# Eight relations around one x in a row of the projection table, read back five vectors at a time

## The reference

```
h_proj = einsum('nd,rde->rne', x, relation_weight)
att    = sum(h_proj[etype, src] * tanh(h_proj[etype, dst] + edge_attr), -1)
a      = softmax of att over the edges of one dst
h_nb   = segment_sum(x[src] * a, dst)
x1     = layernorm(x + leaky((x + h_nb) @ res_w1.T) + leaky((x * h_nb) @ res_w2.T))
feat   = x1 / out_degree
out    = layernorm(x1 + segment_sum(feat[src], dst) / in_degree)
```

## Time and profile before

| | us |
|---|---|
| median of 3 runs | 12504.19 (12502.96 to 12504.48) |
| profiled execution | 12504.09 |
| its span | 12502.3 |
| table stage ends (first load of the next) | 406.11 |
| first gather of the attention stage | 410.66 |
| first instruction of the node stage on VectorE | 8249.73 |
| first gather of the mean stage | 8446.5 |
| POOL / DVE / ACT / PE busy | 9106.9 / 4974.7 / 2167.4 / 1355.6 |

### The profile page before, as it was taken

How to read it: one execution, slowest core, us unless ns; L and a number is a source line. 1 busy time by engine, 2 the same in 40 slices (tenths; PEclk the granted TensorE clock), 3 DMA queues, 4 the chain that set the end, 5 groups by cost and what they waited for, 6 DMA issues and landing times. The chain is left out here.

```text
span 12502.3 us, 36138 instructions
## 1 busy us (share of the span) xinstructions
PE 1355.6 (11%) x4902; PEld 711.9 (6%) x4902; DVE 4974.7 (40%) x4627; ACT 2167.4 (17%) x1796; POOL 9106.9 (73%) x9773
## 2 busy tenths in 40 slices
PE   9311111110101111111111111140000000000001
PEld 3100000000000000000000000040000000000001
DVE  4455555555555555555555555561111111111113
ACT  4111111111111111111111111122222222222221
POOL 1577777777777777777777777757777777777776
PEclk9655555555555555555555555555555555555555
DMA  9422222222222222222222222211222222222222
GB/s 403 174 80 79 79 79 79 80 79 80 79 80 79 80 79 79 79 79 79 79 79 79 79 79 79 77 41 51 53 52 53 52 53 53 52 53 52 53 52 50
DMA packets 456359, 998.94 MB, mean 80 GB/s; under 512 B 189300, under 2 KB 242276, under 8 KB 443412
## 3 DMA queue, kind: packets, MB, share of 16 engines
q0 software_dynamic: 356272, 519.14, 18.2%
q1 hardware_dynamic: 62004, 271.05, 5.6%
q10 hardware_dynamic: 38064, 208.54, 4.2%
HBM read 629.48 MB, written 368.55 MB: 80 GB/s over the span
## 5 line engine op out<-in xcount | busy, mean ns | idle before, releaser
L1044 POOL DMA_INDIRECT gy<-ytab,idx x3125 | 2948.3, 943 | 999.6 <-issue 952.1
L817 POOL DMA_INDIRECT gs<-table,idx_s x3125 | 2953.3, 945 | 971.3 <-issue 971.3
L820 POOL DMA_INDIRECT gd<-table,idx_d x3125 | 2948.0, 943 | 951.3 <-issue 951.3
L1077 DVE TENSOR_TENSOR_SCAN run<-keep,add 128x1664 f32<-128x1664 f32 x125 | 452.9, 3623 | 3015.1 <-ACT keep L1101 3015.1
L868 DVE TENSOR_TENSOR banks<-banks,gd 128x1600 f32<-128x1600 f32 x125 | 229.0, 1832 | 3430.4 <-DMA gd<-table,idx_d 3430.4
L1006 PE MATMUL banks<-hi,lo 128*128 128x392 bf16 x3125 | 803.4, 436 | 6984.7 <-DVE hi L855 6984.7
L855 DVE TENSOR_TENSOR hi<-banks,digit 128x9800 bf16<-128x9800 f32 x125 | 1294.3, 10354 | 0.0
L972 ACT ACTIVATE banks<-banks 128x1600 f32<-128x1600 f32 x125 | 186.0, 1488 | 4912.5 <-DVE banks L868 4912.5
L1099 ACT COPY add<-gy 128x1600 f32<-128x1600 f32 x125 | 400.4, 3203 | 2474.2 <-DMA gy<-ytab,idx 2474.2
L1006 PEld LDWEIGHTS banks<-hi,lo 128*128 128x128 bf16 x3125 | 381.4, 126 | 7406.7 <-DVE hi L855 7033.6
L982 ACT COPY rowbuf<-run 128x1625 f32<-128x1625 f32 x125 | 410.2, 3282 | 776.4 <-DVE run L895 776.4
(11 more groups left out here) (184 smaller groups left out, 2402.7 us busy)
## 6 DMA issues: line engine op xcount, KB each, us to landing
table<-rows SPq DMA_DIRECT2D x98, 1536.0 KB, 9.4
sums<-rowbuf ACTq DMA_DIRECT2D x125, 825.0 KB, 3.7
ef<-in_edge_attr_dram SPq DMA_DIRECT2D x125, 800.0 KB, 4.9
sums<-rowbuf ACTq DMA_DIRECT2D x125, 800.0 KB, 3.5
gs<-table,idx_s POOLq DMA_INDIRECT x3125, 2.6
gd<-table,idx_d POOLq DMA_INDIRECT x3125, 2.4
gy<-ytab,idx POOLq DMA_INDIRECT x3125, 2.4
ytab<-y SPq DMA_DIRECT2D x7, 448.0 KB, 3.5
```

What stands on the lines that cost most here:

```text
L817: pool.indirect_dma_start(out=gs[:, s, g, :], out_offset=None, in_=table, in_offset=bass.IndirectOffsetOnAxis(ap=idx_s[:, s, g:g + 1], axi ...
L820: pool.indirect_dma_start(out=gd[:, s, g, :], out_offset=None, in_=table_third, in_offset=bass.IndirectOffsetOnAxis(ap=idx_d[:, s, g:g + 1 ...
L1044: pool.indirect_dma_start(out=gy[:, s, g, :], out_offset=None, in_=ytab, in_offset=bass.IndirectOffsetOnAxis(ap=idx[:, s, g:g + 1], axis=0 ...
L1077: nc.vector.tensor_tensor_scan(run[:, :, :].rearrange("p w t -> p (w t)"), keep[:, :, :].rearrange("p w t -> p (w t)"), add[:, :, :].rearr ...
```

## The change

- The table row is now eight relations around one x: [r0 r1 r2 r3 x r4 r5 r6 r7], 576 floats, four rows a node. Storage shrinks from 48 to 36 vectors a node. The copies of x shrink from 16 to 4 a block: VectorE two, ScalarE one, GpSimd one.
- A gather for the source takes five vectors: either [r0..r3, x] or [x, r4..r7]. VectorE multiplies and sums all five (x too) and picks the right one by three bits of the relation, in three predicated copies; a fourth, over 25 x 64 elements, brings x to one place. `edge_rows` has 11 short operations instead of five, and the three bits are kept until `back`.
- The node of block b in partition j is now j*98 + b, so x is loaded with one long piece per partition; the store of a block goes to 128 places that lie 98 blocks apart. For the node stages x is read again in the old order (node b*128 + j), by SyncE at the head of the attention node stage.
- Weights: even quarters of a row on partitions 0 to 63, odd ones on 64 to 127, loaded by eight DMAs; the matmuls of a block alternate between the halves, each with a contraction of 64 rows. The clearing of the lower half is gone.
- In the table stage only the first 50 columns of src, dst and type are loaded; the rest comes at the head of the attention stage. The rest of x is held until the weights are in.
- Clears at the head of both edge stages shrink to the columns that are read, and ScalarE no longer waits for them. The last chunk makes no indices.

```diff
-        table = nc.dram_tensor("table", (NPAD * R // 2, 3 * D), F32).ap()
+        table = nc.dram_tensor("table", (NPAD * R // 8, 9 * D), F32).ap()
+        table_vec = table.rearrange("a (b d) -> (a b) d", b=9)
...
-            nc.vector.scalar_tensor_tensor(out=idx_s[:, s, :], in0=src_sb[:, at], scalar=float(R // 2),
-                                           in1=half[:, :], op0=ALU.mult, op1=ALU.add)
+            nc.vector.scalar_tensor_tensor(out=idx_s[:, s, :], in0=src_sb[:, at], scalar=float(9 * R // 8),
+                                           in1=near[:, :], op0=ALU.mult, op1=ALU.add)
...
+                    sp.dma_start(xs[0:P - 1, 0:FIRST, :], x_rows[:, 0:FIRST, :]).then_inc(x_first, 16)
...
+                    sp.wait_ge(w_in, 128)
+                    sp.dma_start(xs[0:P - 1, FIRST:, :], x_rows[:, FIRST:, :]).then_inc(x_in, 16)
...
-                    sp.dma_start(src_sb[:, 0:T], src.rearrange("(p t) -> p t", p=P)).then_inc(idx_in, 16)
+                    sp.dma_start(src_sb[:, 0:SOON], src_v[:, 0:SOON]).then_inc(idx_in, 16)
...
+                        sp.dma_start(table_by_part[:, bass.ds(b, 1), :],
+                                     rows[:, s:s + 1, :, :].rearrange("p o r c -> p o (r c)")).then_inc(stored[s], 16)
...
+                            u, h = k // 2, k % 2
+                            nc.tensor.matmul(ps_p[k][:, :], xbT[64 * h:64 * h + D, s, :],
+                                             w_all[64 * h:64 * h + D, 2 * u:2 * u + 2, :, :].rearrange("d q c e -> d (q c e)"),
...
+                        vec = gs[:, s, :, :].rearrange("p g (c d) -> p g c d", c=5)
                         nc.vector.tensor_tensor(prod[:, :, :, :], arg.unsqueeze(2).to_broadcast([P, G, 2, D]),
-                                                gs[:, s, :, :].rearrange("p g (c d) -> p g c d", c=3)[:, :, 0:3:2, :],
-                                                ALU.mult).then_inc(ef_free, 1)
+                                                vec[:, :, 0:5:4, :], ALU.mult)
+                        nc.vector.tensor_tensor(vec[:, :, 1:4, :], arg.unsqueeze(2).to_broadcast([P, G, 3, D]),
+                                                vec[:, :, 1:4, :], ALU.mult).then_inc(ef_free, 1)
...
+                        nc.vector.tensor_reduce(att_of[:, 0:5:4, :].rearrange("p c g -> p g c"), prod[:, :, :, :], AX.X, ALU.add)
+                        link.then(nc.vector.tensor_reduce(att_of[:, 1:4, :].rearrange("p c g -> p g c"), vec[:, :, 1:4, :], AX.X, ALU.add))
+                        link.then(nc.vector.copy_predicated(att_of[:, 0:4, :], right[:, s, :].unsqueeze(1).to_broadcast([P, 4, G]),
+                                                            att_of[:, 1:5, :]))
+                        nc.vector.tensor_copy(side, right[:, s, :])
+                        link.then(nc.vector.copy_predicated(att_of[:, 0:2, :], high[:, s, :].unsqueeze(1).to_broadcast([P, 2, G]),
+                                                            att_of[:, 2:4, :]))
...
+                        link.then(nc.vector.copy_predicated(gs[:, s, :, 4 * D:5 * D],
+                                                            side.unsqueeze(2).to_broadcast([P, G, D]), gs[:, s, :, 0:D]))
...
+        xs = sb(ctx, "xs", [P, NB, D])
+                sp.wait_ge(x_pad, 1)
+                sp.dma_start(xs[:, 0:NB - 1, :], x[0:(NB - 1) * P, :].rearrange("(b j) d -> j b d", j=P)).then_inc(x_in, 16)
...
+                    if not later(i):
+                        dve.wait_ge(x_in, 32)
```

More of the change, by code:

```diff
@@ L539, in gnn_program @@
         half = sb(ctx, "half", [P, G], I32)
+        quad = sb(ctx, "quad", [P, G], I32)
+        near = sb(ctx, "near", [P, G], I32)
+        right = sb(ctx, "right", [P, 2, G], I32)
+        low = sb(ctx, "low", [P, G], I32)
+        high = sb(ctx, "high", [P, 2, G], I32)
         odd = sb(ctx, "odd", [P, 2, G], I32)
@@ L552, in gnn_program @@
         tail = sb(ctx, "tail", [P, RW])
+        SOON = 2 * G
+        src_v, dst_v, type_v = (v.rearrange("(p t) -> p t", p=P) for v in (src, dst, etype))
         def edge_rows(link, c, s):
@@ L711, in _ @@
                 def _(act):
-                    act.dma_start(w_all[0:D, :, :], rel_w.rearrange("r d e -> d r e")).then_inc(w_in, 16)
+                    w_v = rel_w.rearrange("(q h c) d e -> h q d c e", h=2, c=4)
+                    for h in range(2):
+                        for q in range(RQ):
+                            act.dma_start(w_all[64 * h:64 * h + D, q, :, :], w_v[h, q]).then_inc(w_in, 16)
                     def take_x(b, k, s):
@@ L721, in quarters @@
                         take_out(act, nc.scalar.copy, 1, b, s, i)
-                        nc.scalar.copy(rows[:, s, RP - POOL_DUP - ACT_DUP:RP - POOL_DUP, D:2 * D],
+                        nc.scalar.copy(rows[:, s, RQ - POOL_DUP - ACT_DUP:RQ - POOL_DUP, 4 * D:5 * D],
                                        xs[:, bass.ds(b, 1), :].to_broadcast([P, ACT_DUP, D]))
@@ L880, in back @@
                         if later(c):
                             dve.wait_ge(rows_ready, c)
[L882 removed]
+                        nc.vector.tensor_reduce(att_of[:, 0:5:4, :].rearrange("p c g -> p g c"), prod[:, :, :, :], AX.X, ALU.add)
+                        link.then(nc.vector.tensor_reduce(att_of[:, 1:4, :].rearrange("p c g -> p g c"), vec[:, :, 1:4, :], AX.X, ALU.add))
+                        nc.vector.tensor_copy(add[:, :, 0], run[:, :, G])
@@ L899, in back @@
                         last.then_inc(run_ready, 1)
-                        edge_rows(link, c + 2, s)
-                        assert link.n == PER_CHUNK, link.n
+                        if not later(c):
+                            dve.wait_ge(rest_in, 48)
+                        if not last_one:
+                            edge_rows(link, c + 2, s)
+                            assert link.n == PER_CHUNK, link.n
                     def chunk(c, s, i):
@@ L1061, in _ @@
                     stage(1, 1)
-                    nc.vector.memset(keep[:, :, :], 0.0).then_inc(init_done, 1)
-                    nc.vector.memset(add[:, :, :], 0.0).then_inc(init_done, 1)
-                    link.then(nc.vector.memset(run[:, :, :], 0.0))
+                    nc.vector.memset(keep[:, :, 0], 0.0)
+                    link.then(nc.vector.memset(run[:, :, G], 0.0))
                     def chunk(c, s, i):
```

109 lines of the change are left out of this document (56 added, 53 removed).

## The result

The changed kernel takes 12520.65 us (median of 20 runs, 12520.11 to 12522.15), the kernel before beside it 12503.05 (12502.03 to 12504.99): ratio 1.0014, 95% interval 1.0008 to 1.0020. Forecast were 12420 us, a gain of 84, with a range of 12395 to 12482; measured is a loss of 18, small but clear of the noise. The profiled execution has a span of 12519.8 us, 17.5 over that of before.

The account below looks back on a forecast made before the run. Table stores were taken to bound the kernel up to 406 us, then POOL's back-to-back gathers. 12504.1 - 100 (table) + 3 (gathers) + 11.7 (last chunk) + 1 (node-stage x) = 12420 us, range 12395 to 12482.

Parts of the forecast that it names:

- the arrival of x: Table stage: x, 3.05 MB in 24 KB pieces, takes 7.3 us at 416 GB/s and is in at about 15 us.
- slow stores: Rival, table stage: scattered stores run at the old pace and only the early start stays, 13 us, 12507; chance 0.03.
- TensorE as the bound: Rival, table stage: TensorE replaces the stores as bound at 3.56 us a block, stage ends 60 us later, 12480; chance 0.22.
- Store pace 2.84 us a block: Table stage: smaller rows cut the stores from 370.5 to 277.9 us, 2.84 a block; stage left at 306, -100 us.
- TensorE, two halves side by side: Table stage: matmuls on the two partition halves overlap, eight in 1.7 us, 2.3 us a block with the transpose.
- The drain: Table stage: tiling-mode changes around each transpose drain TensorE, 0.43 us on each side, 3.2 us a block, total 12455.
- Gathers +3: Gathers: 3125 of them widen from 768 to 1280 bytes, costing 0 to 6 us, taken as +3.
- the rival of wider gathers: Rival, gathers: wider rows cost POOL more in a step, 50 ns a gather or 156 us, 12576; chance 0.04.
- VectorE +13.3 us a chunk: Attention stage: wider product and sum, the pick of x and small operations add 13.3 us a chunk, hidden in 124 chunks.
- Tail +11.7: Last attention chunk: no gathers cover VectorE's extra 13.3 us; less the indices no longer made, +11.7 us.
- The rival that the pick holds POOL: Rival, attention gathers: the pick or another new VectorE operation holds POOL every chunk, 229 to 400 us slower; chance 0.07.
- x in the node stage +1: Node stage: rereading x takes 15.5 us, hidden before its first reader; later gathers may cost 0 to 4, taken as +1.

Follow-up runs that it names:

- e1: Changed kernel with both loads of x over 127 partitions cut into partitions 0 to 111 and 112 to 126: 13868.93 us, 0.9936 of the kernel before.
- e12: e1 run again on a chip with gathers of 1.25 us: 12427.26 us against 12512.66 for the kernel before, 0.9932.
- e2: Changed kernel with only the long load of x cut, into partitions 0 to 121 and 122 to 126: 13915.62 us, 0.9969 of the kernel before.
- e3: Kernel before with its long load of x cut into partitions 0 to 126 and partition 127: 14112.59 us, 1.0111 of the kernel before.
- e8: e1 with full-height projection matmuls, zeros in the other half of the weights: 13942.48 us, 0.9990 of the kernel before.
- e5: e1 with src, dst and type loaded in full in the table stage instead of 50 columns: 13883.10 us, 0.9947 of the kernel before.
- e18: e1 with the mask of the pick of x in SBUF instead of PSUM, gathers of 1.25 us: 12496.24 us, 0.9994 of the kernel before.
- e11: e1 with all gs gathers first and wide bit picks, masks in SBUF, while gd arrives: 13732.69 us, 1.0975 of the kernel before.
- e17: e11 with flag copies into PSUM replacing the memsets and the picks' masks read from PSUM: 12404.91 us, 0.9921 of the kernel before.
- e15: Same kernel as e18, on a chip with gathers of 1.40 us: 13871.13 us, 0.9939 of the kernel before.
- e4: e1 with each block's matmuls in the order upper, upper, lower, lower: 13869.12 us, 0.9936 of the kernel before.
- e6: e1 without holding the long load of x until the weights are in: 13879.77 us, 0.9944 of the kernel before.

## Why the prediction was wrong

**The step that failed** is the arrival of x: "x comes in 24 KB pieces (3.05 MB, 7.3 us at 416 GB/s)" and "So x is in at about 15 us". The rate was that of stores over 128 partitions, all sixteen engines busy. The load covers 127, moves 28 GB/s and is in at 127 us. The table stage gained 100 us by its pace and lost 105 in this hole: 410.97 instead of 306. e1 and e12 take the fault away and the rest comes out (308.13); e2 halves it; e3 makes it in the kernel before. Shown, then, from three sides. Nothing in the trace of before could price it, since all its large transfers span 128 or 64 partitions, but the cue stood in the diff: `xs[0:P - 1, ...]`. That the kernel is slower, to which the prediction gave 0.10, is no credit to it: its case for slower was a held POOL, and the 0.06 for a time near that of before stood on slow stores and on TensorE as the bound; none of these happened. The Trainium skill has the rule too, and I didn't weigh it: "DMA: Bandwidth & Descriptors", Why a DMA increments its semaphore by 16 and not by 1, says that the number of engines is the largest one up to 16 that divides the slowest dimension of both sides, and gives 127 partitions as its example for 1. The traces agree: DMA share 0.07 with 127 partitions, 0.13 and half the wait with 122.

**The other steps**, with what they measured:

- Store pace 2.84 us a block: 1152 KB at 409 to 413 GB/s, 2.86 to 2.88. Right, so scattered stores don't run slower, and that rival is out. First store at 15: 14.36 with the load cut. It needs only the short load of the first blocks; the long one is in at 24.49 even so, not at 15, which costs little because the stores of blocks 0 to 3 run meanwhile.
- TensorE, two halves side by side, "eight take four times 0.43 = 1.7 us": 1.99. The reading of the earlier trace rows was right, and e8 shows what it is worth (61 us of stage). The drain that the prediction priced by the Trainium skill, "TensorEngine Tiling (Array Packing)", Key Properties, at 0.43 us on each side and 3.2 us a block, isn't seen at that size: the stores stayed the bound. What may be left of it is small: the first half-height pass starts 0.23 us behind the transpose's start (median of 52 blocks of e12), a full-height one 0.11 us (e8). The allowance of 6 us for ramp, transposes and scattered stores was 8.
- Gathers +3: +1.2. The 512 bytes more cost POOL nothing (946 ns as before); the rival of wider gathers is out.
- The rest of the indices behind the first gathers, nothing, and 12 us without that cover: 11.5 to 13 (e5).
- VectorE +13.3 us a chunk: 5.15 and 5.14 for product and sum, 1.93 for the pick where I took 1.83, and its wait for gd went from 27.43 to 14.7 us a chunk on average, 14.08 in the last (forecast 14). Tail +11.7: +11.4. Two slips of the text changed nothing: the upper bound of 3.2 us for the pick is not twice 1.83, and 512 bytes more on 128 partitions are 66 KB a pair of gathers and not 102; the DMA share rose to 0.38 (forecast 0.36).
- The rival that the pick holds POOL, taken as 0: right, and e18 shows that the mask in PSUM, which the prediction gave as a reason, is what decides. With the mask in SBUF the same instruction costs 0.6 us a chunk, near the 0.67 from which the rival was to decide; its price in the prediction (the pick's whole length) was too high for a pick of 1.9 us, for only the part from the next gather's start counts.
- x in the node stage +1: 0; its first reader doesn't wait for it.

With the load cut, the forecast gain of 84 us stands against 85 (e12) and 90 (e1). That isn't luck of cancelling terms: e12's first gather is 97.6 us earlier than before, and with the +1.2 and +11.4 measured in after that gives -85.0. One term was wrong, and it was the whole gain.

## What to carry to other kernels

Count the partitions of every large transfer that a change adds: 112 + 15 rows cost 10 us where 127 cost 110. A DMA share of 0.06 to 0.08 with all engines idle is the mark that a transfer on one engine leaves in these traces. Where POOL issues gathers back to back, keep the mask of a long predicated copy beside them in PSUM; and where x, weights and stores meet in the queues, hold the large pieces until the small ones that start the pipeline are in.

## What the runs showed of the hardware

- A predicated copy with mask and data in SBUF keeps a gather back until 0.78 us behind its end (e11, e18); with the mask in PSUM the gathers keep their 0.94 us (e12, e17). What that costs depends on the chip: 78 us where a gather takes 1.25 us, nothing where it takes 1.40 (e18, e15). The cause of the second kind of chip stays open.
- TensorE runs passes on different row halves side by side out of the order of the program (e4), but the engine that takes quarter 1 out gets it only behind quarter 2, which stands ahead of it in the program.
- Small pieces starve beside 24 KB pieces: the weights come at 22.26 us instead of 7.96 (e6).
- One DMA engine alone moves 28 GB/s in 24 KB pieces and 18 GB/s in pieces of 256 bytes (e3), where sixteen move 206 in such pieces: in small pieces it does more alone than its sixteenth, 13 GB/s.
